# Reordering the last slots of a user-history attention kernel: lone blocks, late folds, and an earlier power on GpSimd

## What is computed

```python
mean_hist = (hist_items * maskf[..., None]).sum(1) / (maskf.sum(1, keepdims=True) + 1e-06)
q = mean_hist @ Wq.T
k = jnp.einsum('btd,ed->bte', hist_items, Wk)
v = jnp.einsum('btd,ed->bte', hist_items, Wv)
scores = jnp.einsum('bd,btd->bt', q, k) * scale + jnp.log(decay + 1e-12)
scores = jnp.where(hist_mask, scores, -jnp.inf)
attn = jax.nn.softmax(scores, axis=-1)
long_term = jnp.einsum('bt,btd->bd', attn, v)
# short_term: mean of the last 5 valid items; g: a sigmoid gate of their popularity and age
user = g * short_term + (1.0 - g) * long_term
mu = user.mean(-1, keepdims=True)
var = user.var(-1, keepdims=True)
return (user - mu) / jnp.sqrt(var + 1e-05) * ln_gamma + ln_beta
```

## Time and profile before

| what | us |
|---|---|
| median of 3 runs | 186.98 |
| the profiled execution, its own time | 185.14 |
| the profiled execution, span from first to last instruction | 183.4 |
| TensorE matmul busy (x2795) | 157.3 |
| VectorE busy | 152.2 |
| GpSimd busy | 142.9 |
| ScalarE busy | 121.6 |

### The profile page before, as it was taken

How to read it: one execution, slowest core, us unless ns; L and a number is a source line. 1 busy time by engine, 2 the same in 40 slices (tenths; PEclk the granted TensorE clock), 3 DMA queues, 4 the chain that set the end, 5 groups by cost and what they waited for, 6 DMA issues and landing times.

```text
span 183.4 us, 8117 instructions
## 1 busy us (share of the span) xinstructions
PE 157.3 (86%) x2795; PEld 125.0 (68%) x2795; DVE 152.2 (83%) x1289; ACT 121.6 (66%) x706; POOL 142.9 (78%) x106
## 2 busy tenths in 40 slices
PE   5869767298999999999999999999969996819990
PEld 5748656267677778887877788868838884518660
DVE  4559742999399999999999999999999999857043
ACT  2010777277688889879688898978868989551220
POOL 6817899999997979899999999999978969371001
PEclk9956999969999999999999999999999999985997
DMA  4899999999999999999999999999998302000000
GB/s 108 279 420 364 308 409 395 408 408 412 416 427 405 402 350 388 407 403 412 412 417 406 375 372 406 416 413 418 404 383 313 131 4 73 4 16 0 4 0 14
DMA packets 8008, 55.48 MB, mean 303 GB/s; under 512 B 2080, under 2 KB 3360, under 8 KB 4000
## 3 DMA queue, kind: packets, MB, share of 16 engines
q1 hardware_dynamic: 7152, 53.59, 74.4%
q0 software_dynamic: 576, 1.33, 2.1%
q10 hardware_dynamic: 240, 0.05, 0.2%
HBM read 54.70 MB, written 0.26 MB: 300 GB/s over the span
## 4 chain that ended last, share of the span: by engine, by line
PE 48%; POOL 21%; issue 17%; DVE 5%; DMA 4%; ACT 3%; SPq 1%; POOLq 0%; ACTq 0%
PE ps_acc L445 18%; PE ps_acc L453 14%; POOL gprod L349 13%; PE ps_query L478 5%; DMA x<-in_r_hist_items_dram 4%; POOL mblk L326 3%; DVE junk_v L915 3%; PE ps_acc L469 2%; PE ps_group L464 2%; PE ps_group L492 2%; PE ps_group L493 2%; POOL pblk L337 2%; PE ps_acc L457 1%; ACT gprod L591 1%; POOL hide_s L386 1%
## 5 line engine op out<-in xcount | busy, mean ns | idle before, releaser
L915 DVE SCALAR_TENSOR_TENSOR junk_v<-x,ps_query 128x128 f32<-128x128 f32 x548 | 121.6, 278 | 4.8 <-ACT query L625 4.7
L349 POOL TENSOR_TENSOR gprod<-x,query 128x1024 f32<-128x1024 f32 (+1 forms) x32 | 75.0, 2345 | 13.2 <-ACT query L625 12.0
L591 ACT ACTIVATE gprod<-gprod 128x128 f32<-128x128 f32 x252 | 74.3, 301 | 13.5 <-POOL gprod L349 13.1
L445 PE MATMUL ps_acc<-x,mblk 128*16 128x128 f32 x1600 | 57.2, 281 | 3.5 <-DMA x<-in_r_hist_items_dram 3.5
L453 PE MATMUL ps_acc<-x,pblk 128*32 128x256 f32 x768 | 52.7, 385 | 4.0 <-issue 2.3
L445 PEld LDWEIGHTS ps_acc<-x,mblk 128*16 128x16 f32 x1600 | 46.3, 99 | 6.9 <-issue 2.7
L591 ACT ACTIVATION_READ_ACCUMULATOR gprod<-gprod 128x1 f32 x252 | 48.5, 193 | 0.0
L915 DVE DVE_READ_ACCUMULATOR junk_v<-x,ps_query 128x1 f32 x548 | 44.4, 81 | 0.0
L453 PEld LDWEIGHTS ps_acc<-x,pblk 128*32 128x32 f32 x768 | 27.9, 111 | 17.4 <-issue 6.8
L337 POOL TENSOR_TENSOR pblk<-own,ex 128x800 f32<-128x800 f32 (+1 forms) x16 | 24.2, 1510 | 6.2 <-ACT ex L636 6.0
L326 POOL TENSOR_TENSOR mblk<-own,mask_f 128x800 f32<-128x800 f32 (+1 forms) x17 | 24.9, 1472 | 0.1
(11 more groups left out here) (112 smaller groups left out, 153.7 us busy)
## 6 DMA issues: line engine op xcount, KB each, us to landing
x<-in_r_hist_items_dram SPq DMA_DIRECT2D x31, 1600.0 KB, 10.2
x<-in_r_hist_items_dram SPq DMA_DIRECT2D x1, 832.0 KB, 8.2
x<-in_r_hist_items_dram SPq DMA_DIRECT2D x1, 768.0 KB, 6.0
decay_s<-in_r_hist_age_hours_dram SPq DMA_DIRECT2D x4, 100.0 KB, 13.2
out_dram<-y SPq DMA_DIRECT2D x4, 64.0 KB, 3.9
mask_u<-in_r_hist_mask_dram SPq DMA_DIRECT2D x1, 100.0 KB, 7.3
wq<-in_L_rec_Wq_dram SPq DMA_DIRECT2D x1, 64.0 KB, 7.2
wk<-in_L_rec_Wk_dram SPq DMA_DIRECT2D x1, 64.0 KB, 7.7
```

Source lines behind the costliest of these rows:

```text
L349: nc.gpsimd.tensor_tensor(gprod[:, t, 0:k * D].rearrange("p (r d) -> p r d", d=D), rows(at(s, t), ROWS - k, ROWS), query[:, s % 2, t, :].u ...
L445: ins = nc.tensor.matmul(dst[c:c + TU, 0:D], blk[:, s % 2, t, m, :], x[:, at(s, t), m * D:(m + 1) * D], start=(m < CG), stop=(m >= ROWS - CG))
L591: ins = nc.scalar.activation(src, src, ACT.Copy, accum_out=score[:, s % 2, t, at_row:at_row + 1])
L915: ins = V.scalar_tensor_tensor(out=junk_v[:, t, r, :], in0=x[:, at(s, t), r * D:(r + 1) * D], scalar=1.0, in1=c_query[t], op0=ALU.mult, op ...
```

## The change

It acts on the slots from 31 on, and on no earlier one.

- Tiles 28 and 29 no longer share a block instruction: GpSimd builds two blocks of 400 elements in place of one of 800, and does the power of group 2 and the products of tile 31 ahead of them.
- TensorE folds pair 13 after the weighted sum of tile 29 (slot 35), pair 14 after that of tile 31 (slot 37), and pair 15 in slot 38 as before.
- ScalarE copies the weighted sum of tile 27 ahead of the products' sums of tile 31.
- The exponential of tile 31 is written ahead of the copy of slot 37 and no longer after the copy of slot 36; both places are between the copies of tiles 29 and 30.
- VectorE writes `y` of group 2 at the fifteenth dot of tile 31, no longer at the second.
- `weighted_blocks` counts the lone blocks from tile 28 on.

```diff
+FIRST_LONE = NTILE - 2 * PAIR
+FOLD_AFTER = {NTILE + 3: LAST_PAIR - 2, NTILE + 5: LAST_PAIR - 1, NTILE + 6: LAST_PAIR}
...
-            return n // PAIR + 1 if n < NTILE - 1 else NPAIR + 1
+            return n // PAIR + 1 if n < FIRST_LONE else FIRST_LONE // PAIR + 1 + n - FIRST_LONE
...
-                if n == NTILE:
-                    build_pblk(w + 1)
-                elif w == LAST_TILE - 1:
+                if w == LAST_TILE - 1:
                     build_pblk(w, 1)
-                elif tile(w) and w % PAIR == 0 and w // PAIR < LAST_PAIR - 1:
+                elif tile(w) and w % PAIR == 0 and w < FIRST_LONE:
                     build_pblk(w)
...
                 if tile(n - 1) and query_slot(n - 1) == n:
                     products(n - 1)
+                if n == NTILE:
+                    build_pblk(FIRST_LONE, 1)
+                    build_pblk(FIRST_LONE + 1, 1)
...
-                if n == NTILE + 2:
-                    fold_pair(w // PAIR - 1)
...
-                if n != NTILE + 2 and tile(w - 1) and w % PAIR == 0:
+                if n <= NTILE and tile(w - 1) and w % PAIR == 0:
                     fold_pair(w // PAIR - 1)
+                if n in FOLD_AFTER:
+                    fold_pair(FOLD_AFTER[n])
...
+                if n == NTILE + 2:
+                    sum_products(LAST_TILE, 0, ROWS - DOTS_LAST)
                 if n == NTILE + 3:
                     exponential(LAST_TILE - 1)
-                if tile(w):
+                if n == NTILE + 5:
+                    exponential(LAST_TILE)
+                if tile(w) and n != NTILE + 2:
                     copy_weighted(w)
-                if n == NTILE + 4:
-                    exponential(LAST_TILE)
...
-                if n > LEAD and tile(n - 2):
+                if n == NTILE + 1:
+                    copy_weighted(w + 1)
+                elif n > LEAD and tile(n - 2):
                     sum_products(n - 2, 0, ROWS_AHEAD)
...
-                    if i == 1 and k == 0 and has(g, 2, NGROUP):
+                    if i == (1 if g < NGROUP else DOTS - 3) and k == 0 and has(g, 2, NGROUP):
                         finish_scale(g - 1)
```

## The result

The changed kernel takes 180.82 us (median of 4 runs, 180.38 to 181.24). The kernel before has 188.13 us over the 4 runs that stand beside these. The ratio is 0.9685, with a 95% interval of 0.963 to 0.974: 3.1% faster, where 181.1 us and 3.1% were forecast. The profiled execution took 181.13 us, its span, which answers to the earlier trace rows, is 179.4.

A forecast was written before the change was run, and what follows sets the result against it. One chain of dependent steps bounds the end: last weighted sum 6.9 us earlier, minus 1.0 for the fold behind it, net 5.9 off the 186.98 us median gives 181.1 us; range 179.9 to 184.0.

The forecast's parts named there:

- The stall of the fold on the copy of tile 27: TensorE's fold of pair 13 waited for ScalarE's copies, 5.3 us in two waits, one of 4.2; the latter would go.
- The split 4.6 + 1.3: Of 5.9 us net gain, about 4.6 from tile 31's exponential no longer held back, 1.3 from VectorE's wait for the power.
- What is late next: On VectorE, masking of tile 30 needs ScalarE's sums: starts about 161.8, before 163.38, so 1.6 of 2.5 us gained.
- The chain of VectorE: VectorE from masking tile 30 to masking tile 31: 4.18 us before, y now inside it adding at most 0.35, taken as 0.3.
- The fold behind the last weighted sum: TensorE's fold of pair 14, now after the last weighted sum, costs 1.0 us there, bounds 0.8 to 1.0.
- TensorE's slack: TensorE ends tile 30 at 167.3 and waits 1.2 us for VectorE's last block before the last weighted sum.
- "Ahead of a copy" moves nothing: ScalarE's last exponential stays between the copies of tiles 29 and 30; its new place was costed at nothing.
- a fall in the new gap of 1.2 us: Rival: TensorE's clock falls to 1.2 GHz in its pause before the last weighted sum, +3.1 us, 184.2 us; chance 0.10.
- a gap of 1.82 us that had left the clock at 1.00: TensorE's earlier gap at 134.3 left the clock at 1.00; cited against the clock falling in the new, shorter gap.
- the prediction's own signs of being wrong: A window at 0.50, the last weighted sum following tile 30 at once, or tile 31's exponential after the copy of 29.

The follow-up runs named there:

- the third run of the changed kernel: The changed kernel run again without an edit, its third profile: median 180.59 us, ratio 0.966 to the kernel before; 17.25 us from GpSimd's tile 30 products to the group's copy.
- experiment 6: The changed kernel without GpSimd's order and VectorE's later y, so moved folds and earlier copy only: median 181.88 us, ratio 0.9777 to the kernel before.
- the two profiles that kept the clock: The changed kernel run twice more without an edit, clock at 1.00 throughout: medians 180.87 and 180.59 us, ratios 0.9665 and 0.966 to the kernel before.
- the first execution: The changed kernel's first profiled execution, no further edit, clock lost from 156.8 to 163.6: took 181.13 us; ratio of its runs to the kernel before 0.9685.
- experiment 4: The kernel before with only GpSimd's order (power and products of 31 first, split block) and VectorE's later y: median 183.85 us, ratio 0.9824.

## Why the prediction was right

- *The stall of the fold on the copy of tile 27.* Right, and shown twice, by the folds alone and by the copy alone. Each would have done. The prediction never said that the parts replace each other; it priced only the whole.
- *The split 4.6 + 1.3.* The folds alone gave 4.66 and GpSimd's order with y 1.34 on top, both with VectorE's lag taken off. What is late next was also right: the masking of tile 30 waited for ScalarE's sums, 1.20 us, and came 6.68 us into the end (163.65 - 156.97) where before it came at 8.25, 1.6 earlier as forecast.
- *The chain of VectorE.* From masking to masking 4.44 us against 4.18 in before: y costs 0.26 among the dots, the forecast took 0.3.
- *The fold behind the last weighted sum.* From that sum's start to the group's copy 3.82 us (174.22 - 170.40) against 2.95: 0.87, inside the 0.8 to 1.0 given.
- *TensorE's slack.* 1.30 us against 1.2.
- *"Ahead of a copy" moves nothing.* Both kernels have the exponential of 31 between the copies of 29 and 30; in the third run of the changed kernel it starts 0.03 after VectorE's transposition (168.99 + 0.21), with ScalarE idle 2.36 us before. In experiment 6 it stands at its old place and starts 0.04 after the transposition (169.42 + 0.21, start 169.67), so the place makes no difference there either.
- *What was wrong:* the place of the clock. The forecast weighed a fall in the new gap of 1.2 us, and took a gap of 1.82 us that had left the clock at 1.00 as evidence that such a gap is safe. Its window stops where that gap ends; the trace reads 1.00 behind it too, up to 146 us, so the evidence stood, but it was one gap. In the profiled execution the clock fell after the old gap of 1.39 us ahead of tile 26. There TensorE and not VectorE was the bound, and two of the prediction's own signs of being wrong are in that profile: windows at 0.50, and the last weighted sum following tile 30 at once. Tile 28 started 9.18 us after tile 26, in place of 6.25 and 5.99 in the two profiles that kept the clock. Of these 3.2 us about half was taken up by TensorE's waits, above all the 1.30 us ahead of the last weighted sum, and the end was 1.6 us longer than in the third profile (18.87 against 17.25). VectorE was 1.05 us later in the same execution, which alone would have made it 18.30 (an estimate, 17.25 + 1.05); beside that the lost clock added 0.6.
- *Where it was lucky:* the sum prices one case, VectorE's lag as in before and the clock kept, and only the third profile is that case. In the first execution the end fell by 4.35 us and not by 5.9. And the forecast of the time starts from a median of 3 runs (186.98) that the fourth run moved to 188.13, so agreement to 0.3 us in the time is closer than the spread of the runs warrants.

## What to carry to other kernels

When one wait holds back a whole list, several edits each remove it; price them together against the next limit, not one by one and added. Before a small step is moved away from a wait, see whether the wait still exists once its producer has moved: y at its old place would have been free. And measure a change to the last 25 us from a fixed instruction near it: the times varied by 3 us for reasons that lie ahead of it, which hid differences of 1 us that the profiles show plainly.

## What was not expected of the hardware

The same gap of 1.36 to 1.42 us ahead of tile 26's weighted sum stands in twelve profiles. In eleven the clock stayed at 1.00 behind it; in one it fell to 0.50 within 1.3 us of TensorE's return, and stayed there for 6.8 us of work without a pause. So what a gap costs can't be read from one profile. Nor does its length alone order the cases here: 1.71 us ahead of tile 28 (experiment 6) left the clock at 1.00, and 1.98 us (experiment 4, with a gap of 1.33 us shortly before it) was followed by 0.50. The Trainium skill, page TensorE: Matmul & The Clock Gate, Part 1, says that the point at which the clock rises once matmuls are under way varies from run to run. That is about the rise; here it was the fall that came in one execution and not in others.

VectorE's lag behind GpSimd at the start of the end was 4.22 to 5.34 us over the fourteen profiles, with the same instructions ahead of it. Where it comes from was not tried.
